# Decoder layer in fp32: routing's down product from rounded halves, attention's maxima spread over other rounds, a store moved in SyncE's queue

## The reference

```python
x = layernorm(x + self_attention(x, ...))             # 16 heads of 32, masked, 2048 x 2048 scores
x = layernorm(x + cross_attention(x, ctx, mask, ...)) # 154 context rows
x = layernorm(x + moe(x))

def moe(x):                                           # T = 4096 tokens
    scores = sigmoid(x @ gate_weight.T)               # 64 experts
    topk_idx, topk_w = grouped_top_8(scores + e_bias) # 4 of 8 groups, then 8 experts
    out = sum over the 8 experts of topk_w * expert(x)  # capacity 512 a expert, hidden 256
    shared = silu(x @ shared_gate.T) * (x @ shared_up.T) @ shared_down.T   # hidden 512
    return out + shared
```

## Time and profile before

| | |
|---|---|
| median of 3 runs | 3286.88 us (3275.59 to 3287.71) |
| profiled execution | 3281.05 us, its span 3279.3 us |
| TensorE, ScalarE busy | 90%, 44% of the span |
| VectorE, GpSimd busy | 62%, 46% |
| mean granted TensorE clock | 0.961 |

### The profile page before, as it was taken

How to read it: one execution, slowest core, us unless ns; L and a number is a source line. 1 busy time by engine, 2 the same in 40 slices (tenths; PEclk the granted TensorE clock), 3 DMA queues, 4 the chain that set the end, 5 groups by cost and what they waited for, 6 DMA issues and landing times. The chain is left out here.

```text
span 3279.3 us, 59175 instructions
## 1 busy us (share of the span) xinstructions
PE 2963.8 (90%) x19197; PEld 1934.0 (59%) x19197; DVE 2039.8 (62%) x4795; ACT 1453.1 (44%) x3375; POOL 1520.5 (46%) x1093
## 2 busy tenths in 40 slices
PE   7998999989989999898988979999799994999992
PEld 4444444444444444444434468888688883888882
DVE  4645646556465574554725568888477774777776
ACT  1443544434444444444442257777322222555551
POOL 3343443424434344243452234444377774665656
PEclk8999999999999999999999989999999996999996
DMA  4223022221221212212207522222222224999997
GB/s 114 62 64 82 7 74 79 58 63 32 75 78 44 66 44 74 78 31 67 66 30 253 189 84 88 79 82 84 84 71 68 68 61 140 258 254 259 257 254 265
DMA packets 185030, 343.33 MB, mean 105 GB/s; under 512 B 36136, under 2 KB 54696, under 8 KB 183848
## 3 DMA queue, kind: packets, MB, share of 16 engines
q1 hardware_dynamic: 135336, 250.90, 25.7%
q0 software_dynamic: 28800, 48.43, 6.8%
q10 hardware_dynamic: 20736, 41.95, 3.3%
HBM read 206.96 MB, written 83.89 MB: 89 GB/s over the span
## 5 line engine op out<-in xcount | busy, mean ns | idle before, releaser
L548 ACT ACTIVATE sa_probs<-sa_s 128x512 f32<-128x512 f32 (+3 forms) x1280 | 609.8, 540 | 692.9 <-PE sa_s L440 353.1
L334 POOL TENSOR_TENSOR sa_both<-sa_probs 128x2048 f32<-128x2048 f32 (+2 forms) x160 | 590.0, 3687 | 628.4 <-ACT sa_probs L548 616.9
L406 PE MATMUL sa_w<-sa_parts 96*128 96x512 f32 (+3 forms) x1280 | 515.0, 440 | 81.7 <-DVE sa_pmax L607 43.2
L440 PE MATMUL sa_s<-sa_parts 128*128 128x512 f32 (+3 forms) x1280 | 480.4, 409 | 27.3 <-ACT sa_probs L548 21.4
L607 DVE CUSTOM_DVE_ANT_0 sa_w<-sa_w,sa_maskS 128x512 f32<-128x512 f32 (+3 forms) x512 | 327.5, 649 | 238.7 <-PE sa_w L406 234.2
L406 PEld LDWEIGHTS sa_w<-sa_parts 96*128 96x128 f32 x1280 | 232.3, 195 | 409.4 <-issue 202.5
L611 DVE TENSOR_REDUCE sa_pmax<-sa_w 128x1 f32<-128x512 f32 (+3 forms) x768 | 422.7, 585 | 47.1 <-PE sa_w L406 44.0
L440 PEld LDWEIGHTS sa_s<-sa_parts 128*128 128x128 f32 x1280 | 242.0, 193 | 168.1 <-ACT sa_probs L548 96.6
L1519 POOL DMA_INDIRECT token_and_weight_of_slot<-rt_entry,rt_sl x256 | 261.0, 1020 | 124.4 <-issue 91.3
L458 PE MATMUL sa_pv<-sa_probs,sa_values 128*32 128x512 f32 (+3 forms) x2560 | 284.2, 538 | 0.0
L1252 ACT ACTIVATE xa_sm<-xa_sm,xa_nmax 128x154 f32<-128x154 f32 x512 | 209.4, 414 | 54.9 <-DVE xa_nmax L1175 54.9
(11 more groups left out here) (236 smaller groups left out, 5360.0 us busy)
## 6 DMA issues: line engine op xcount, KB each, us to landing
list_w<-in_w SPq DMA_DIRECT2D x138, 512.0 KB, 5.6
sa_parts<-early_halves SPq DMA_DIRECT2D x384, 128.0 KB, 2.4
early_xt<-in_xT SPq DMA_DIRECT2D x32, 1024.0 KB, 5.7
scratch_attention_T<-sa_oT SPq DMA_DIRECT2D x32, 256.0 KB, 2.4
on_at<-scratch_attention_T SPq DMA_DIRECT2D x32, 256.0 KB, 3.1
on_xr<-in_x SPq DMA_DIRECT2D x32, 256.0 KB, 3.4
scratch_x<-on_xn ACTq DMA_DIRECT2D x32, 256.0 KB, 2.1
scratch_x_T<-on_xnT ACTq DMA_DIRECT2D x32, 256.0 KB, 3.4
```

Source lines behind the costliest of these rows:

```text
L334: pool.tensor_tensor(both[:, p % 2, :, 0:w], probs[:, even, :, 0:w], probs[:, odd, :, 0:w], ALU.add).then_inc(both_ready, 1)
L406: nc.tensor.matmul(ps[:, 0:w], qparts[0:3 * HD, h, q0:q0 + P], kparts[0:3 * HD, h, k0:k0 + w], start=True, stop=True).then_inc(work_ready, 1)
L440: mm = nc.tensor.matmul(ps[:, 0:w], kparts[:, h, kb * P:(kb + 1) * P], qparts[:, h, q0:q0 + w], start=True, stop=not diag)
L548: nc.scalar.activation(probs[:, r % NPB, h, 0:w], sbank[n % NSB][:, 0:w], ACT.Exp).then_inc(exp_done, 1)
```

## The change

- `EARLY` becomes 24, and the maxima follow one table: chunk 1's last 8 in rounds 0 and 1, chunk 2's 48 in rounds 3 to 9 (before 4 to 9), chunk 3's 64 in rounds 10 to 21 (before 12 to 21), the next iteration's chunk 0 in rounds 30 to 34 (before 31 to 34) and 24 of its chunk 1 in rounds 35 to 39 (before 16 in 36 to 39). Round 2 has none. The values product of chunk 3 moves from round 6 to round 14.
- SyncE waits for the first score of the iteration in place of the last weighted sum of the one before, and stores chunk 3 of the iteration before behind the spread of chunk 2.
- In routing the down product takes three products of fp32r halves. ScalarE rounds hT into the high half, GpSimd subtracts for the low half, ahead of its scatters of the tile before; hT has one buffer instead of two, its halves two. The down weights are split once, by ScalarE and VectorE, ahead of the first tile.

```diff
+    MAXIMA = ((1, EARLY, 32, 0, 2), (2, 0, 48, 3, 10), (3, 0, 64, 10, 22), (0, 0, 16, 30, 35), (1, 0, EARLY, 35, 40))
     def maxima_in(c, k):
-        if c == 0:
-            return spread_over(1, EARLY, 32, 0, 3, k)
-        if c < NC - 1:
-            return spread_over(c + 1, 0, len(segments(c + 1)), 0, rounds(c) - 2, k)
-        return spread_over(0, 0, 16, 7, 11, k) + spread_over(1, 0, EARLY, 12, 16, k)
+        r = first_round[c] + k
+        keys = []
+        for of, i0, i1, r0, r1 in MAXIMA:
+            if r0 <= r < r1:
+                n, m = i1 - i0, r1 - r0
+                keys += [("m", of, i) for i in range(i0 + n * (r - r0) // m, i0 + n * (r + 1 - r0) // m)]
+        return keys
...
-                 (1, 0): [("k", 3)], (1, 1): [("q", 3)], (1, 2): [("v", 3)], (1, 7): [("s", 2)],
+                 (1, 0): [("k", 3)], (1, 1): [("q", 3)], (2, 2): [("v", 3)], (1, 7): [("s", 2)],
...
-                sp.wait_ge(pv_done, it * NR + NPB)
+                sp.wait_ge(s_ready, it * NU + 1)
                 apart(sp, passed)
                 spread_parts(it, 2)
+                if it > 0:
+                    store(it - 1, 3)
...
                 store(it, 2)
-                store(it, 3)
             each_group(sp, body)
+            store(ITERS - 1, 3)
...
+                def low_half(t, s):
+                    pool.wait_ge(hT_high, t + 1)
+                    pool.tensor_tensor(hTh[:, s, 1], hT[:], hTh[:, s, 0], ALU.subtract).then_inc(hT_low, 1)
+
+                low_half(0, 0)
                 pool.wait_ge(table_set, 16)
                 def body(t, s):
+                    if before_end(t, 1):
+                        low_half(t + 1, 1 - s)
...
                 def down(t, s):
-                    pe.wait_ge(hT_done, t + 1)
+                    if isinstance(t, int) and t == 0:
+                        pe.wait_ge(wd_high, 1)
+                        pe.wait_ge(wd_low, 1)
+                    pe.wait_ge(hT_high, t + 1)
+                    pe.wait_ge(hT_low, t + 1)
                     wait(pe, r_done, t - 1)
-                    for k in range(KT):
-                        mm = nc.tensor.matmul(dd[s][:], hT[:, s, k], wd[:, k], start=k == 0, stop=k == KT - 1)
+                    for n, (a, b) in enumerate(TERMS):
+                        for k in range(KT):
+                            mm = nc.tensor.matmul(dd[s][:], hTh[:, s, a, k], wdh[:, b, k], start=k == 0 and n == 0,
+                                                  stop=k == KT - 1 and n == len(TERMS) - 1)
                     mm.then_inc(dn_done, 1)
...
+                def high_half(t, s):
+                    act.wait_ge(hT_done, t + 1)
+                    wait(act, dn_done, t - 1)
+                    nc.scalar.copy(hTh[:, s, 0], hT[:]).then_inc(hT_high, 1)
+                act.wait_ge(early.mlp_in, 48)
+                nc.scalar.copy(wdh[:, 0], wd[:]).then_inc(wd_high, 1)
...
                 def act_part(t, s):
                     dve.wait_ge(hg_done, t + 1)
-                    wait(dve, dn_done, t - 1)
-                    dve.tensor_tensor(hT[:, s].rearrange("p k t -> p (k t)"), hg[:], uu[s][:], ALU.mult).then_inc(hT_done, 1)
+                    wait(dve, hT_low, t)
+                    dve.tensor_tensor(hT[:].rearrange("p k t -> p (k t)"), hg[:], uu[s][:], ALU.mult).then_inc(hT_done, 1)
...
+                dve.wait_ge(early.mlp_in, 48)
+                dve.wait_ge(wd_high, 1)
+                dve.tensor_tensor(wdh[:, 1], wd[:], wdh[:, 0], ALU.subtract).then_inc(wd_low, 1)
```

More of the change, by code:

```diff
@@ L76, in self_attention @@
     round_at = [(c, k) for c in range(NC) for k in range(rounds(c))]
-    EARLY = 16
-    def spread_over(c, i0, i1, k0, k1, k):
-        if not k0 <= k < k1:
-            return []
-        n = i1 - i0
-        return [("m", c, i) for i in range(i0 + n * (k - k0) // (k1 - k0), i0 + n * (k + 1 - k0) // (k1 - k0))]
-    def maxima_in(c, k):
-        if c == 0:
-            return spread_over(1, EARLY, 32, 0, 3, k)
-        if c < NC - 1:
-            return spread_over(c + 1, 0, len(segments(c + 1)), 0, rounds(c) - 2, k)
-        return spread_over(0, 0, 16, 7, 11, k) + spread_over(1, 0, EARLY, 12, 16, k)
+    EARLY = 24
+    MAXIMA = ((1, EARLY, 32, 0, 2), (2, 0, 48, 3, 10), (3, 0, 64, 10, 22), (0, 0, 16, 30, 35), (1, 0, EARLY, 35, 40))
+    def maxima_in(c, k):
+        r = first_round[c] + k
[5 more added lines that the diff above has]
+        return keys
     def others_in(c, k):
         table = {(0, 0): [("k", 2)], (0, 1): [("q", 2)], (0, 2): [("v", 2)], (0, 3): [("s", 1)],
-                 (1, 0): [("k", 3)], (1, 1): [("q", 3)], (1, 2): [("v", 3)], (1, 7): [("s", 2)],
+                 (1, 0): [("k", 3)], (1, 1): [("q", 3)], (2, 2): [("v", 3)], (1, 7): [("s", 2)],
                  (2, 11): [("s", 3)],
@@ L1379, in route_and_shared @@
 def route_and_shared(nc, sems, x2, x2T, early, gateT, ebias, res, table, unused, lists):
+    TERMS = ((0, 0), (0, 1), (1, 0))
     with ExitStack() as ctx:
@@ L1396, in route_and_shared @@
         xT = sb("xT", [P, 2, KT, P]); xr = sb("xr", [P, 2, DM])
-        hg = sb("hg", [P, DM]); hT = sb("hT", [P, 2, KT, P])
+        hg = sb("hg", [P, DM]); hT = sb("hT", [P, KT, P]); hTh = sb("hTh", [P, 2, 2, KT, P], F32R); wdh = sb("wdh", [P, 2, KT, DM], F32R)
         r = sb("r", [P, 2, DM])
@@ L1415, in route_and_shared @@
         gate_done = sem("gate_done"); gu_done = sem("gu_done"); pos_done = sem("pos_done"); dn_done = sem("dn_done")
-        sc_done = sem("sc_done"); hg_done = sem("hg_done"); hT_done = sem("hT_done")
+        sc_done = sem("sc_done"); hg_done = sem("hg_done"); hT_done = sem("hT_done"); hT_high = sem("hT_high"); hT_low = sem("hT_low"); wd_high = sem("wd_high"); wd_low = sem("wd_low")
         pick = sem("pick"); sel_done = sem("sel_done"); wden_done = sem("wden_done"); place = sem("place"); kk_done = sem("kk_done"); k8_done = sem("k8_done")
@@ L1580, in up, with body @@
                     nc.scalar.activation(hg[:], gg[s][:], ACT.Silu).then_inc(hg_done, 1)
-                each_tile(act, up)
+                def high_half(t, s):
[4 more added lines that the diff above has]
+                nc.scalar.copy(wdh[:, 0], wd[:]).then_inc(wd_high, 1)
+                def body(t, s):
+                    up(t, s)
+                    high_half(t, s)
+                each_tile(act, body)
             @block.vector
```

## The result

The changed kernel takes 3300.9 us (median of five runs, 3298.2 to 3307.5), beside 3286.9 for the kernel before: 1.0059 times as long, 95% interval 1.0039 to 1.0080. Slower, as forecast; but by 14 to 19 us where I had written 43, and the time lies inside the range. The profiled executions differ by 17.1 us of span, 3296.4 against 3279.3.

What follows compares the result with a forecast made beforehand. GpSimd, tied with TensorE, was taken to end routing; self-attention had one large hole an iteration. Routing +35 and attention +11 gave +46 on 3281.05 us: 3327, by the runs' median 3333; predicted 3330, range 3293 to 3370.

Steps and rivals of the forecast that it cites:

- Rival B: Routing: the subtract is hidden beside the scatters, so routing gives -4 and the kernel takes 3294; chance 0.12.
- rival C: Routing: TensorE's idling lowers its clock, costing 32 x 1.3 = +42 us more, 3372; chance 0.10.
- Sum: 30 x 1.33 - 4.6 = +35 us: Routing: 30 GpSimd subtracts between scatters at 1.33 us each, less 4.6 us of true waiting; ends +14 and +60.
- the hole: Self-attention, each iteration after the first: TensorE's 4.09 us wait in round 2 plus lower clock behind it, 6.7 us.
- T + 11.0: Self-attention: when chunk 2's last transfer lands, counted from T, the end of q's product; TensorE then waits 4.9 to 5.5 us.
- my +1.1: Self-attention, each iteration: the new wait with lower clock costs 7.8 us against the old hole's 6.7.
- +11: Self-attention's sum: +8 for iteration 0's new wait, +3 for the prologue's extra maxima, net 0 for seven iterations.
- Rounds 4 to 9 get 6.9 maxima a round for 8: Self-attention: fewer maxima a round wait less for VectorE, taking back 1.1 us an iteration, net 0.
- Its ends, -10 and +30: Self-attention's bounds: -10 with waits shorter by 3 and clock loss hidden, +30 with the longer wait and nothing won back.
- my sum, +46: Whole kernel: +35 us in routing and +11 in self-attention.
- 2.6 us an iteration: Self-attention: time lost to the lower clock behind the wait, within the hole's 6.7 us and the new wait's 7.8.
- rival A: Self-attention: chunk 2's parts land by T + 6, the hole closes, giving back 47 us; 3270 in all; chance 0.06.

Runs made afterwards that it cites:

- exact_down: The changed kernel with the exact down product of four 128x512 products again, rounding and subtract kept but their halves unread: 3304.8 us, ratio 1.0067 to the kernel before.
- twice_sub: The changed kernel with GpSimd doing the low half's subtract twice, the extra one into a tile nobody reads: 3342.3 us, ratio 1.0181 to the kernel before.

## Why the prediction was right and wrong

**Right: GpSimd ends routing, and the subtract lies on its path.** Rival B (the subtract hidden) and rival C (the clock falls) are out: the 12 ns that a scatter shortens by give back 2.9 of 38.5 us, and the granted clock is 0.99. The weight split is hidden as forecast, since VectorE's first choosing instruction stands 7.0 us behind the stage's start (7.2 before), and ScalarE's copy of hT takes 0.62 us for my 0.6.

**Too large: "Sum: 30 x 1.33 - 4.6 = +35 us".** Measured +28.4. The instruction was 1.28, not 1.33: I added 0.05 for dispatch, and the trace shows the opposite, 0.08 us of overlap with what stands behind it. The idle time was as read (4.9 for 4.6). The rest is scatters that became 12 ns shorter each, 2.9 us, which no row of before could tell. The estimate of 1.12 us from the Trainium skill ("GPSIMD Engine Reference", section 3.1), "by which this sum would be +29 us", comes near the total for another reason: the instruction took 1.28 us, and there the measurement decides. TensorE's down product took 2.82 us for my 2.6 and saved 0.70 a tile where I wrote 0.92; off the path, it changed nothing, as exact_down shows. I also divided VectorE's 263.2 us by 32 tiles, though its window of 355.8 us holds 30.6: 8.6 a tile and not 8.2, which still left it room.

**Right: the hole is exchanged, not closed.** T + 11.26 for T + 11.0, a wait of 5.01 us, the lower clock behind it. Rounds 2 and 3, which hold the wait, grew by 1.7 us against my +1.1; the wait was as forecast (5.0 to 5.8 us, 5.2 on average, from iteration 1 on), and the clock's loss, which I had taken as equal behind both waits, was larger: 7.7 us at 0.59 on average instead of 0.70 is an estimate of 0.8 us more. With round 4, which got shorter, the stretch q2 to k3 grew by 0.85. Iteration 0 and the prologue: +7.3 by the queries of iteration 1, against +11.

**Wrong, the step that failed: "Rounds 4 to 9 get 6.9 maxima a round for 8 and should wait less for VectorE; I take back 1.1: net 0 for seven iterations".** The net was -2.3 us an iteration in the profiled execution and -1.6 in others: beside the +1.7 of the hole, 3.9 (in others some 3.3) came back and not 1.1. By the rounds: with the values product left in place, rounds 4 to 9 won 2.0 us for my 1.1 and rounds 10 to 23 lost 0.5 (43.59 to 41.55, 56.65 to 57.13); the product's move is worth another 0.7 at most. The rest I had put at nothing: 1.0 in rounds 0 and 1, which hold 8 maxima for 10, and 0.7 in rounds 30 to 39, which hold 8 more than before and are shorter all the same. There I counted maxima and not where they stand among the other products: 1.1 us of it is round 33's interruption, another 1.1 in rounds 30 and 31 is open, and the eight more maxima take back 1.5 behind them. So attention came to -9 by the spans (-4 by the time of its half alone) where I wrote +11. Its ends, -10 and +30, held it, at their edge. Of the 29 us between my sum, +46, and the spans' +17 attention is thus 20, routing 6 and the untouched rest 3. With 28.4 - 9.1 the +17 is found to within 2 us, the rest of the kernel's -3.2 and routing's ends of +1.1 between them.

I had costed the clock at 2.6 us an iteration; no run measures its share apart. And rival A's condition ("a landing at T + 6") was the wrong question: it is not the landing that had to come earlier but the first use that had to come a round later.

## What to carry to other kernels

Where two engines are tied, saving on one is worth nothing, and moving its work onto the other costs in full: here 28 us for an instruction that fits free of charge on a third engine. When filling work is brought forward into a hole, ask for its data first; one round later was worth 35 us. And small fillers have a price that depends on where they stand: four maxima cost some 0.2 us between scores that another engine paced, and 1.15 between weighted products. Before costing a new spread, read from the timeline what the same filler takes in each of its places, and count round by round.

## What the runs showed of the hardware

**VectorE held up beside GpSimd.** VectorE's small product of 128x64 takes 224 ns, at most 242 in the kernel before. In the changed kernel (instructions by tile, ns min/median/max, and the one that meets the subtract above):

```profile
L1641 DVE TENSOR_TENSOR rt_tmp<-rt_sfc,rt_gm x32: 224/225/2077, 2330.2 to 2714.5; 128x64 f32<-128x64 f32 x32
```

```profile
2511.73 2.06 DVE L1641 TENSOR_TENSOR rt_tmp<-rt_sfc,rt_gm 128x64 f32<-128x64 f32 x1
2513.93 0.23 DVE L1644 MAX8 rt_t<-rt_tmp 128x8 f32<-128x64 f32 x1
```

It starts before GpSimd's subtract (2512.42 to 2513.70) and ends 0.09 us behind it; 13 of the 32 are like this one, 2.05 to 2.08 us long, and its mean in the loop is 1037 ns. With two subtracts in a row (twice_sub) it takes up to 3.28 us and again ends 0.09 behind the second. With the subtract on VectorE the longest is 295 ns. The Trainium skill, "SBUF — State Buffer", section "SBUF: two separate sides", has a VectorE instruction with two inputs from SBUF and a GpSimd instruction exclude one another for the length of the whole instruction. The trace agrees in that the small product is held until the subtract's end. The section also has the one that starts first go first, and by the recorded starts that was VectorE's; why it lost is open. A scatter was under way on GpSimd when it started (2511.42 to 2512.40), but beside scatters alone the same product took 242 ns at most in the kernel before. In this kernel it cost nothing, as VectorE had room.

**The place of a small matmul has a price of its own.** In rounds 32 and 33 four 96-row maxima of 256 columns cost 1.15 us between weighted products and some 0.2 between scores, beside ScalarE's exponentials of 0.50 us each. I had costed such products by their count.
